# Expert layer of a perceiver-style network: weight rows dealt to partitions in neighbouring groups, with stationary operands taken at a step of four and eight columns

## The reference, cut to what matters

```python
# T = 512 tokens, d = 512, E = 16 experts, H = 1024, top 2
logits = xt @ Wr + br
probs = jax.nn.softmax(logits, axis=-1)
w, idx = jax.lax.top_k(probs, TOP_K)
...
h = gelu(einsum('td,edh->teh', xt, W1) + b1)      # W1 (16, 512, 1024)
o = einsum('teh,eho->teo', h, W2) + b2            # W2 (16, 1024, 512)
y = xt + einsum('teo,te->to', o, comb)
```

## Time and profile before

| what | us |
|---|---|
| median of 3 runs | 2500.89 |
| lowest and highest run | 2499.41, 2500.94 |
| the profiled execution | 2503.7 |
| its span in the trace | 2501.8 |
| expert stage in the trace, about | 1383.7 to 1720 |

### The profile page before, as it was taken

How to read it: one execution, slowest core, us unless ns; L and a number is a source line. 1 busy time by engine, 2 the same in 40 slices (tenths; PEclk the granted TensorE clock), 3 DMA queues, 4 the chain that set the end, 5 groups by cost and what they waited for, 6 DMA issues and landing times. The chain is left out here.

```text
span 2501.8 us, 57450 instructions
## 1 busy us (share of the span) xinstructions
PE 2273.9 (91%) x21752; PEld 1489.4 (60%) x22035; DVE 1821.4 (73%) x3365; ACT 1579.5 (63%) x2934; POOL 1150.1 (46%) x905
## 2 busy tenths in 40 slices
PE   6899999999999999998888699995899899998796
PEld 3456656665666656666445577773567676776442
DVE  5678878887888867776363699995777777767336
ACT  5556666666666666665234499993477677788423
POOL 4546676667666665554100000003467676656420
PEclk9999999999999999998899799997999999999897
DMA  6323432233322321124321699994534433324102
GB/s 207 96 60 93 125 91 65 68 88 102 93 74 71 102 79 39 38 61 154 114 106 40 218 367 362 366 329 145 170 121 123 130 117 115 98 90 146 64 1 86
DMA packets 248819, 313.58 MB, mean 125 GB/s; under 512 B 63312, under 2 KB 174544, under 8 KB 247648
## 3 DMA queue, kind: packets, MB, share of 16 engines
q1 hardware_dynamic: 244592, 301.75, 37.4%
q10 hardware_dynamic: 3312, 6.03, 0.6%
q0 software_dynamic: 640, 2.10, 0.3%
HBM read 226.23 MB, written 47.91 MB: 110 GB/s over the span
## 5 line engine op out<-in xcount | busy, mean ns | idle before, releaser
L585 POOL TENSOR_TENSOR a_late<-a_late 128x512 bf16<-128x512 f32 x272 | 315.9, 1162 | 358.7 <-ACT a_late L645 358.1
L981 PE MATMUL ps<-w,a_xhi 128*128 128x512 bf16 x1081 | 411.3, 380 | 9.2 <-POOL a_xlo L552 3.1
L982 PE MATMUL ps<-w,a_xhi 128*128 128x512 bf16 x1086 | 413.1, 380 | 0.4
L983 PE MATMUL ps<-w,a_xlo 128*128 128x512 bf16 x1071 | 407.4, 380 | 0.1
L2182 POOL TENSOR_TENSOR a_plo<-a_p,a_phi 128x512 bf16<-128x512 f32 x256 | 306.6, 1198 | 178.1 <-ACT a_phi L2219 168.9
L611 ACT ACTIVATE a_kraw<-ps 128x256 f32<-128x256 f32 x272 | 104.2, 383 | 366.4 <-PE ps L983 364.6
L2314 DVE CUSTOM_DVE_ANT_0 a_junk<-ps,a_biasrow 128x512 bf16<-128x512 f32 x256 | 176.2, 688 | 115.0 <-PE ps L2454 89.1
L2214 ACT ACTIVATE a_p<-ps,a_mcol 128x512 f32<-128x512 f32 x256 | 174.8, 683 | 87.5 <-PE ps L2472 79.9
L723 DVE TENSOR_TENSOR a_v<-ps,a_v 128x256 bf16<-128x256 f32 x272 | 114.4, 421 | 152.0 <-ACT a_v L613 150.4
L737 DVE SCALAR_TENSOR_TENSOR a_kraw<-a_kraw,a_rn 128x1024 f32<-128x1024 f32 (+1 forms) x80 | 155.2, 1940 | 80.8 <-POOL a_rn L536 80.8
L536 POOL TENSOR_TENSOR a_rn<-a_rn,a_power 128x16 f32<-128x16 f32 (+1 forms) x80 | 205.0, 2563 | 6.7
(11 more groups left out here) (470 smaller groups left out, 6845.4 us busy)
## 6 DMA issues: line engine op xcount, KB each, us to landing
e_wst<-in_L_ffn_W SPq DMA_DIRECT2D x46, 2048.0 KB, 10.6
a_ks<-a_khi SPq DMA_DIRECT2D x256, 64.0 KB, 2.0
a_ks<-a_klo SPq DMA_DIRECT2D x256, 64.0 KB, 2.0
a_ct<-in_ctxT SPq DMA_DIRECT2D x16, 1024.0 KB, 5.9
a_ks<-k1h_d SPq DMA_DIRECT2D x128, 128.0 KB, 2.5
xa<-in_ctx SPq DMA_DIRECT2D x8, 1024.0 KB, 5.5
a_xn<-in_ctx SPq DMA_DIRECT2D x8, 1024.0 KB, 5.9
k1h_d<-a_khi SPq DMA_DIRECT2D x64, 128.0 KB, 1.8
```

The source lines that it names most:

```text
L585: pool.tensor_tensor(p_lo[:, m % 3, :], p32[:, m % 2, :], p_hi[:, m % 3, :], ALU.subtract)\
L981: pe.matmul(out, x_hi[:, c, tile], w_hi[:, c, g, :], start=(c == 0), stop=False)
L982: pe.matmul(out, x_hi[:, c, tile], w_lo[:, c, g, :], start=False, stop=False)
L983: last = pe.matmul(out, x_lo[:, c, tile], w_hi[:, c, g, :], start=False, stop=(c == C - 1))
```

## The change

The rows of a weight matrix are dealt out differently: partition `p` now gets the 4 neighbouring rows `4p` to `4p + 3` of W1, and the 8 neighbouring rows `8p` to `8p + 7` of W2. Either is one piece of 16 KB in DRAM. In SBUF the tiles have the shape and size that they had.

Because block `c` of W1 now holds every fourth input feature, `gather` must deliver tokens in that order: its stationary operand takes every fourth column of `x_hi` or `x_lo` (`c:D:C`, a step of 8 bytes in bf16). Because block `m` of W2 holds every eighth hidden feature, `up` must produce them so: its stationary operand takes every eighth column of the weights (a step of 16 bytes). The bias table is laid out on the host to match, with the same shape. The numbers of DMAs, matmuls, weight loads, copies and waits don't change, nor does any order.

```diff
-    w1_d = t["L0_ffn_W1"].rearrange("e (c p) n -> e p c n", p=P)
-    w2_d = t["L0_ffn_W2"].rearrange("e (c p) n -> e p c n", p=P)
+    w1_d = t["L0_ffn_W1"].rearrange("e (p c) n -> e p c n", p=P)
+    w2_d = t["L0_ffn_W2"].rearrange("e (p c) n -> e p c n", p=P)
...
-                            last = pe.matmul(ps[:, bank, c * P:(c + 1) * P], src[:, b, c * P:(c + 1) * P],
+                            last = pe.matmul(ps[:, bank, c * P:(c + 1) * P], src[:, b, c:D:C],
                                              G[:, q % 2, b, :], start=(b == 0), stop=(b == B - 1))
...
-                    cols = slice(m * P, (m + 1) * P)
+                    cols = slice(m, HID, CH)
                     for c in range(C):
                         pe.matmul(out, w1(w_hi, q)[:, c, cols], xe_hi[:, q % 2, c, :], start=(c == 0), stop=False)
...
-        "moe_b1_col": a["L0_ffn_b1"].reshape(E, CH, P).transpose(2, 0, 1),
+        "moe_b1_col": a["L0_ffn_b1"].reshape(E, P, CH).transpose(1, 0, 2),
```

## The result

The changed kernel took 2513.11 us (median of 8 runs), the kernel before 2505.96 us (8 runs) on the same occasions. The ratio is 1.0038, with a 95% interval of 1.0023 to 1.0054: slower by 0.4%. Between the medians lie 7 us, and the ends of the interval are 6 and 14 us. The forecast was no change; what came is the first rival, in its mild form. The profiled execution took 2511.87 us, with a span of 2510.0 against 2501.8.

What follows compares the result with a forecast made beforehand. PE was taken to set the pace of the expert loop, with DVE next. The terms -0.3 + 0 + 0 us led to a median of 2500.6 us, range 2496 to 2620, likeliest case 2496 to 2505.

Steps and rivals of the forecast that it cites:

- Part 2: Stepped weight loads of gather and up in the expert loop: between 0 and 5.3 us a tile, taken as 0.
- the cheap end: Lower bound for up's stepped weight loads: 0 cost, with contiguous bf16 loads 27 ns apart and matmuls 55.9 ns apart.
- Rival 1: Stepped weight loads set PE's pace in the expert loop: slower, anywhere from 2510 to 2660 us; chance 0.23.
- dear end: Upper bound for up's stepped loads, 111 ns apart like fp32 loads: 5.3 us more a tile, +119, 2620 us.
- Part 1: Weight loads in larger pieces: 3 to 8% faster, but 0 in the loop; at most 0.27 us at the stage's start.
- Rivals 2 and 3: Expert loop: loads become slower, 2528 us, chance 0.07; or the DMA share is the real bound, 2493 us, chance 0.05.
- rival 4: Loads still cut into 4 and 2 KB rows, packets and time unchanged; shares the forecast's chance of 0.64.
- Part 3: The bias table, with the same shape and the same pieces: 0.
- Gather: Gather's weight loads at a step of 8 bytes, the milder case of up's: cost 0.

Runs made afterwards that it cites:

- the woven order: Against the changed kernel, one gather matmul of the next tile set behind every third up matmul; 2525.99 us, ratio 1.0083 to the kernel before.
- one step for each tile: Against the kernel before, up takes its columns at a step of 1, 2, 4, 8, 16 or 24, changing tile by tile; 2518.10 us, one run.
- gather's step: Against the changed kernel, W2, up and bias table as before; W1's new rows and gather's step of four kept; 2502.9 us, ratio 0.9987.
- step of four: Against the changed kernel, W2 dealt in two halves with 8 KB pieces, up reading every fourth column; 2503.9 us, ratio 0.9990.
- the loop with less compute and the old pieces: Against the kernel before, from the third tile only a quarter of each half converted, one of three up and down products left out; 2467.51 us, one run.

## Why the prediction was wrong, and where it was right

**The step that failed** is the cover of Part 2, "a factor of two is a fair allowance ... and that factor is what hides". The mechanism was written down, with its point of decision (two stepped loads more than 55.9 ns apart) and its price (22 us for a load 10 ns too slow). Only the value taken was off, and with it the term of the sum that stood at 0. A load with a step of eight takes 60 ns, not the 54 that twice 27 allows. It is 4.3 ns too slow, and 2208 loads x 4.3 ns = 9.5 us; the profiles show 9.4 between the first and the last up matmul. The factor of two had no row behind it; it was just what fitted under 55.9, and a factor of 2.4 did not. The true value was near the cheap end, but with PE full there was no margin between "hides" and "costs", and a choice of 0 there needed more than a guess.

**The rule of the page.** By the Trainium skill, page "SBUF — State Buffer", section "Door 1: The DMA port swizzle", one bf16 in each 16-byte line is too little for full bandwidth, and two are enough. The trace agrees in the main: a step of 16 bytes takes 60 ns where a contiguous load takes 25. A step of 8 bytes takes 34 ns, so two in a line aren't quite at full speed here, only fast enough to hide. The rule doesn't say why the price rises again at steps of 16 and 24 columns (62 and 69 ns).

**Rival 1** came true at 1/13 of its dear end: the fp32 load as upper bound (111 ns) was far too high. In those rows the fp32 matmuls stand 0.11 us apart as well, so 111 ns need not even be the load's own pace. The range held the time, the chance of 0.30 for slower was fair, and the forecast was on the wrong side.

**Part 1** was right in every point: 5760 packets (5400 foreseen), the DMA share below 0.99, landings 1.3 us earlier that bring nothing, SP waiting as long as before (101.9 and 93.2 us), 6.5% more speed where the loads set the pace (3 to 8% estimated from the earlier trace rows). Of the store beside large pieces I feared the right thing: 10.3 us where the queue is full and 9.2 with the rows alone, but 5.3 in the changed kernel, all far below the 18 us at which it would matter. Rivals 2 and 3 fell with it, and rival 4 with the packets.

**Part 3**, the bias table, shows nothing, and the row order alone has a ratio of 1.0001.

**Gather** was right: it has a longer record, and 0 cost.

**What I didn't see** are the 1.3 us behind the last up matmul. PE's clock falls to 0.52 there after the 3.6 us pause. Five profiles in which the last tile's loads are slower than 55.8 ns (the changed kernel twice, the steps without the new order of rows, the woven order, one step for each tile) have slow matmuls in this place, none of the four with hidden loads has (before, rows only, gather's step, step of four). The repeated changed kernel shows it too:

```profile
1713.00:1716.00 3.00, 2.62 (x7) 0.50 0.00 0
```

That fits a link with the stretched loads but doesn't show one. In both groups PE does the same 24 down matmuls 0.216 us apart right before the pause, so the stretched ones ended some 5 us ahead of it. The longer loop also moves the pause, from 316 us after the first load of the stage to 324 and more, and no run moves it without stretching the loads. And stretched loads aren't needed for such a fall: in the loop with less compute and the old pieces, whose loads are contiguous, the clock fell to 0.50 at 1504.9 and at 1549.2, just behind pauses of 2.1 and 3.0 us. So the cause stays open. If the fall is put down to the change all the same, the change costs 9.4 us in the loop and 1 to 4 us in the ramp and the tail (stages of 339.4, 340.9 and 342.4 us against 328.6 to 328.9).

## What to carry to other kernels

A stationary operand may be read at a step as long as its load stays shorter than the matmul in front of it: here a step of four bf16 (34 ns) hides beside a 128-column product (55.8 ns) and a step of eight (60 ns) doesn't, so deal the rows in groups that keep the step at four, and the DMA pieces can still be 8 KB. Where an engine is 99.6% busy, a few ns on each of 2208 instructions are 10 us: bound an unknown cost against the slack that is really there, and if "0" only holds under an assumed factor, say the other side is as likely. Larger DMA pieces pay only where something waits for a landing; look for that wait before counting on them.

## What the runs showed of the hardware

- A bf16 weight load of 128 columns at the 2.4 GHz level follows the next at 25, 25, 34, 61, 62 and 69 ns for steps of 1, 2, 4, 8, 16 and 24 elements (25 may be another floor). At the 1.2 GHz level it is 27 ns at a step of 1 and 59 at a step of 8, while the distance of 128-column products doubles. Its record (98, 98, 115, 144, 149, 161 ns) grows in the same order, but by other amounts, and is no measure of the pace.
- At the 1.2 GHz level a step of eight therefore hides: in the first tile of the changed kernel up's matmuls stand 106.7 ns apart, as in the kernel before.
- Nothing here shows loads read ahead by more than one matmul: at a step of eight the first distance behind a 128-column product was 0.03 us and all later ones 0.06, and weaving short loads among long ones saved nothing (61.6 ns on average).
- Weight loads from HBM in 16 KB pieces ran at 427 GB/s, in 4 and 2 KB rows at 401. With the smaller rows SP's DMA instructions themselves took 1.6 to 4.1 us each while the queue was full (one of eleven 0.37), with the larger ones 0.33.
- Open: what makes steps of 16 and 24 dearer than 8; the last 0.33 us a tile of the woven order; and whether the stretched loop has anything to do with the lower clock behind the pause.
